# A recommendation kernel: the query of tile n-1 made between the masked and the weighted sums, gathers behind the products, both ends reordered

## The chip, the cores and the metric

The kernel runs on 1 core of one Trainium2 chip. The metric is the device time of one execution in microseconds (us). Three runs of the kernel before gave 188.56, 187.62 and 184.76 us, a median of 187.62 us.

## The reference, cut to what matters

512 users have 200 history rows of 128 floats each; a mask says which rows count.

```
maskf = mask;  decay = exp(-alpha * age) * maskf
mean  = (items * maskf).sum(1) / maskf.sum(1)             # [512, 128]
q     = mean @ Wq.T;  k = items @ Wk.T;  v = items @ Wv.T
scores = (q . k) / sqrt(128) + log(decay + 1e-12);  attn = softmax over unmasked rows
long  = attn @ v
short = mean of the 5 last valid rows;  g = sigmoid(gate of their mean popularity and age)
out   = layernorm(g * short + (1 - g) * long) * gamma + beta
```

The kernel multiplies Wq and Wk together once (`wqk`), so that a tile's "query" is the user's mean times `wqk` and is compared with the raw items; Wv is applied once per 128 users to the weighted sums.

## The kernel before, in words

**Tiles.** A tile is 16 users: 8 partitions per user, 25 rows of 128 floats on each partition, 1600 KB. There are 32 tiles in 10 buffers `x`; two tiles make a pair, four pairs a group of 128 users. SyncE issues the loads in order (L269 to L274); the load of tile n waits until the weighted sums of tile n-10 are done (`wx_done`).

**One tile, step by step.** TensorE makes masked sums (L430, with the mask blocks `mblk` from GpSimd, L321); ScalarE copies them scaled by the inverse counts (L581); TensorE folds them to the users' means (L454); ScalarE copies the mean (L596); TensorE makes the query (L463) in one of two PSUM banks, for which it first waits until VectorE has finished the tile before last (`dots_done`); ScalarE copies the query to SBUF (L605), which releases the scoring. The 25 rows are scored by two routes at once: VectorE does 17 of them, a multiply with a running sum each (`dots`, L879); GpSimd multiplies the other 8 in one instruction (`products`, L343) and ScalarE sums these row by row (`sum_products`, L570). VectorE then adds the log-decay and finds each user's maximum in five small steps strewn among the next dots (L826 to L852); ScalarE takes the exponential (L616); GpSimd lays the weights out in blocks (`pblk`, L332); TensorE makes the weighted sums (L438, L442), six slots behind the masked ones; ScalarE copies them (L590) and TensorE folds a pair into the group's bank (L477, L478).

**The order is written out by hand.** Every engine runs a function `slot(n)` for n = 0, 1, 2, ... (VectorE a `step` per pair), in program order, and they meet at semaphores only. TensorE's slot n is: masked sums of tile n, weighted sums of tile n-6, query of tile n-1, mean of tile n, fold of a pair; in the first slots the query comes ahead of the weighted sums. In slots 0 to 3 (`LEAD`) a tile's query is made in its own slot. ScalarE's slot n is: copy the weighted sums n-7, copy the mean n-1, the last four row sums of tile n-3, exponentials of a pair in odd slots, copy the masked sums n, the first four row sums of tile n-2, copy the query n-1. GpSimd's slot n: `pblk` of a pair or `mblk` of a pair, in turn, then the products of tile n-1. In the first slots GpSimd also issues eight small indirect loads of popularity and age (L410), two ahead of all slots and one per slot behind the products; once per group, in the slots 6, 14, 22 and 30, an indirect load of the last five rows (L383), with a copy of its offsets ahead of it (L380). The logarithm of the decay is taken by ScalarE in slot 1 (L623, L626), and VectorE's `setup_hide` (L758, L759) waits for it inside the dots of tile 2. VectorE has two more setup stretches (`setup_gate`, L770, and `setup_last_weights`, L787).

**Fillers.** `keep_busy` (L449) issues matmuls without use: 4 behind each of the slots 0 to 5, and in the last slots ahead of the weighted sums of the tiles 28 (8), 30 (3) and 31 (3). One such matmul is two instructions of the trace.

**Group end.** `sum_weights` (L506), the fold, `copy_att` (L636), `make_long` (L513), and VectorE's finish (L888 to L923); then the store of 64 KB.

## Time and profile before

| what | value |
|---|---|
| runs, median | 187.62 us (184.76 to 188.56) |
| the profiled execution | 185.52 us, span of the profile 183.8 us |
| busy PE / DVE / ACT / POOL | 86% / 83% / 66% / 78% of the span |
| mean granted TensorE clock | 0.956 |
| HBM read | 54.70 MB, 299 GB/s over the span |

PE is TensorE, PEld its weight loads, DVE VectorE, ACT ScalarE, POOL GpSimd, SPq the queue of SyncE. The shares are means over the span: all four engines are far busier in the middle than at both ends. The clock column tells the granted clock of TensorE as a share of 2.4 GHz, 0.50 being 1.2 GHz. A line of the timeline gives the start, the duration, and in brackets how long the engine sat idle before and who released it. Instructions of VectorE overlap by part of their length: 17 dots take 17 x 0.209 us from start to start, though each lasts 0.28.

### The profile page before, as it was taken

Reading aid. Unit: us, or ns where it says so; the run is one execution under the profiler, and the core shown is the slowest. Engines: PE = TensorE matmul, PEld = TensorE weight load, DVE = VectorE, ACT = ScalarE, POOL = GpSimd, SP = SyncE. Lnnn points to the kernel's source line nnn. Section 1 sums busy time; section 2 is a strip of 40 time slices with the busy share of each in tenths; the row PEclk is TensorE's granted clock in tenths of the full one; section 3 lists DMA queues with packets and bytes.
Section 4 is the critical chain, followed back from the end, with each engine's and each line's share of the span. In section 5 each row is a group of like instructions: output and inputs, shape, how many; then the busy total and the mean of one; then the engine's idle time right before and its main releaser. Section 6 shows DMA issues by size and latency. Waiting matters only on the chain.

```text
span 183.8 us, 8155 instructions
## 1 busy us (share of the span) xinstructions
PE 158.4 (86%) x2811; PEld 126.6 (69%) x2811; DVE 152.5 (83%) x1281; ACT 121.6 (66%) x714; POOL 144.1 (78%) x110
## 2 busy tenths in 40 slices
PE   5864649879969999999899999997999999497990
PEld 5753546767747688878686888876878878275660
DVE  4569719958893999999999999999999999979303
ACT  2021664747847599888778889894889889577210
POOL 5608967698899598999899999989999995974301
PEclk9999966999995799999999999999999999999997
DMA  4899999999999589999999999999999810200000
GB/s 105 288 416 378 334 423 412 397 416 419 405 368 358 233 306 427 362 362 379 407 428 424 370 382 407 401 410 395 405 399 366 350 35 0 77 16 0 4 0 14
DMA packets 8008, 55.48 MB, mean 302 GB/s; under 512 B 2080, under 2 KB 3360, under 8 KB 4000
## 3 DMA queue, kind: packets, MB, share of 16 engines
q1 hardware_dynamic: 7152, 53.59, 74.4%
q0 software_dynamic: 576, 1.33, 2.1%
q8 instruction: 22, 0.36, 0.8%
q14 instruction: 18, 0.15, 0.2%
q10 hardware_dynamic: 240, 0.05, 0.1%
HBM read 54.70 MB, written 0.26 MB: 299 GB/s over the span
## 4 chain that ended last, share of the span: by engine, by line
POOL 44%; PE 19%; issue 16%; ACT 12%; DMA 4%; DVE 1%; SPq 1%; POOLq 0%; ACTq 0%; DVEq 0%
POOL gprod L343 27%; ACT gprod L570 9%; POOL mblk L321 7%; PE ps_acc L430 7%; PE ps_acc L438 5%; POOL pblk L332 5%; DMA x<-in_r_hist_items_dram 4%; POOL taken L383 2%; PE ps_group L449 1%; PE ps_query L463 1%; ACT query L605 1%; PE ps_acc L454 1%; POOL pop_taken L410 1%; POOL age_taken L410 1%; PE ps_group L477 1%
## 5 line engine op out<-in xcount | busy, mean ns | idle before, releaser
L879 DVE SCALAR_TENSOR_TENSOR junk_v<-x,ps_query 128x128 f32<-128x128 f32 x544 | 121.2, 279 | 12.6 <-ACT query L605 12.5
L570 ACT ACTIVATE gprod<-gprod 128x128 f32<-128x128 f32 x256 | 75.7, 301 | 20.8 <-POOL gprod L343 20.3
L343 POOL TENSOR_TENSOR gprod<-x,query 128x1024 f32<-128x1024 f32 x32 | 76.1, 2379 | 12.0 <-ACT query L605 10.7
L430 PE MATMUL ps_acc<-x,mblk 128*16 128x128 f32 x1600 | 57.8, 282 | 3.2 <-DMA x<-in_r_hist_items_dram 2.7
L438 PE MATMUL ps_acc<-x,pblk 128*32 128x256 f32 x768 | 51.3, 384 | 7.2 <-POOL pblk L332 6.4
L430 PEld LDWEIGHTS ps_acc<-x,mblk 128*16 128x16 f32 x1600 | 46.5, 99 | 7.1 <-issue 3.1
L570 ACT ACTIVATION_READ_ACCUMULATOR gprod<-gprod 128x1 f32 x256 | 49.3, 193 | 0.0
L879 DVE DVE_READ_ACCUMULATOR junk_v<-x,ps_query 128x1 f32 x544 | 44.6, 82 | 0.0
L438 PEld LDWEIGHTS ps_acc<-x,pblk 128*32 128x32 f32 x768 | 27.3, 110 | 19.5 <-issue 6.0
L332 POOL TENSOR_TENSOR pblk<-own,ex 128x800 f32<-128x800 f32 (+1 forms) x17 | 25.1, 1475 | 4.5 <-ACT ex L616 4.4
L321 POOL TENSOR_TENSOR mblk<-own,mask_f 128x800 f32<-128x800 f32 (+1 forms) x17 | 24.9, 1468 | 0.2
L581 ACT ACTIVATE sums<-ps_acc,rcnt_rows 128x128 f32<-128x128 f32 x32 | 11.6, 361 | 14.6 <-PE ps_acc L430 14.5
L463 PE MATMUL ps_query<-wqk,mean_p 128*128 128x128 f32 x64 | 15.9, 330 | 1.9 <-ACT mean_p L596 1.5
L590 ACT ACTIVATE wx<-ps_acc 128x256 f32<-128x256 f32 x32 | 11.9, 371 | 8.1 <-PE ps_acc L442 8.1
L454 PE MATMUL ps_acc<-fold,sums 128*128 128x16 f32 x64 | 10.9, 246 | 6.6 <-ACT sums L581 6.5
L454 PEld LDWEIGHTS ps_acc<-fold,sums 128*128 128x128 f32 x64 | 10.0, 198 | 9.2 <-ACT sums L581 8.2
L463 PEld LDWEIGHTS ps_query<-wqk,mean_p 128*128 128x128 f32 x64 | 9.8, 191 | 8.3 <-issue 6.3
L449 PE MATMUL ps_group<-own_rows 128*128 128x128 f32 x74 | 13.1, 344 | 1.8 <-POOL own_rows L356 1.8
L449 PEld LDWEIGHTS ps_group<-own_rows 128*128 128x128 f32 x74 | 12.2, 255 | 1.8 <-POOL own_rows L356 1.8
L442 PE MATMUL ps_acc<-x,pblk 128*16 128x128 f32 x64 | 12.5, 277 | 0.0
L477 PE MATMUL ps_group<-fold,wx 128*128 128x16 f32 x64 | 12.4, 270 | 0.0
L478 PE MATMUL ps_group<-fold_odd,wx 128*128 128x16 f32 x64 | 12.4, 270 | 0.0
(112 smaller groups left out, 149.8 us busy)
## 6 DMA issues: line engine op xcount, KB each, us to landing
x<-in_r_hist_items_dram SPq DMA_DIRECT2D x31, 1600.0 KB, 9.0
x<-in_r_hist_items_dram SPq DMA_DIRECT2D x1, 832.0 KB, 7.9
x<-in_r_hist_items_dram SPq DMA_DIRECT2D x1, 768.0 KB
decay_s<-in_r_hist_age_hours_dram SPq DMA_DIRECT2D x4, 100.0 KB, 13.1
out_dram<-y SPq DMA_DIRECT2D x4, 64.0 KB, 4.3
mask_u<-in_r_hist_mask_dram SPq DMA_DIRECT2D x1, 100.0 KB, 7.2
wq<-in_L_rec_Wq_dram SPq DMA_DIRECT2D x1, 64.0 KB, 7.2
wk<-in_L_rec_Wk_dram SPq DMA_DIRECT2D x1, 64.0 KB, 7.5
```

Source lines behind the costliest of these rows:

```text
L321: nc.gpsimd.tensor_tensor(mblk[:, s % 2, t:t + tiles, :, :].rearrange("p t r u -> p (t r) u"), own[:, :].unsqueeze(1).broadcast_to([P, til ...
L332: nc.gpsimd.tensor_tensor(pblk[:, s % 2, t:t + tiles, :, :].rearrange("p t r u -> p (t r) u"), own[:, :].unsqueeze(1).broadcast_to([P, til ...
L343: nc.gpsimd.tensor_tensor(gprod[:, t, :].rearrange("p (r d) -> p r d", d=D), rows(at(s, t), DOTS, ROWS), query[:, s % 2, t, :].unsqueeze(1 ...
L430: ins = nc.tensor.matmul(dst[c:c + TU, 0:D], blk[:, s % 2, t, m, :], x[:, at(s, t), m * D:(m + 1) * D], start=(m < CG), stop=(m >= ROWS - CG))
L438: nc.tensor.matmul(dst[c:c + 2 * TU, 0:2 * D], blk[:, s % 2, t, m:m + 2, :].rearrange("p r u -> p (r u)"), x[:, at(s, t), m * D:(m + 2) * ...
L442: return nc.tensor.matmul(dst[c:c + TU, 0:D], blk[:, s % 2, t, m, :], x[:, at(s, t), m * D:(m + 1) * D], start=False, stop=True)
L449: nc.tensor.matmul(dst, turned, turned, start=True, stop=True)
L454: nc.tensor.matmul(mean_cols(s, t), sums[:, t, :], fold[:, :], start=True, stop=True).then_inc(mean_done, 1)
L463: nc.tensor.matmul(c_query[t], mean_p[:, t, :, :].rearrange("p u c -> p (u c)"), wqk[:, :], start=True, stop=True).then_inc(query_done, 1)
L477: nc.tensor.matmul(users, wx[:, s % 2, t, 0:D], fold[:, :], start=True, stop=False)
L570: ins = nc.scalar.activation(src, src, ACT.Copy, accum_out=score[:, s % 2, t, DOTS + r:DOTS + r + 1])
L879: ins = V.scalar_tensor_tensor(out=junk_v[:, t, r, :], in0=x[:, at(s, t), r * D:(r + 1) * D], scalar=1.0, in1=c_query[t], op0=ALU.mult, op ...
```

## The change

- `early = True`: TensorE makes the query of tile n-1 right behind the masked sums of tile n in every slot, ahead of the weighted sums of tile n-6.
- `LEAD` goes from 4 to 6: the tiles 4 and 5 also get their query in their own slot. In slot 6 no query and no products are made. ScalarE sums all eight product rows of the tile before in one go in these slots, and the exponentials of tiles 0 and 1 come at the end of slot 4.
- The logarithm of the decay moves from the end of slot 1 to slot 2, ahead of the row sums.
- GpSimd issues the eight small indirect loads two per slot in slots 0 to 3, behind the products, and no longer waits for the row numbers ahead of slot 0. The first group's load of rows moves from slot 6 to slot 4; all four read their offsets straight from `first_row`, without the copy and the wait on it.
- The last tile has 21 rows on VectorE and 4 on GpSimd and ScalarE. Its weight block is made by VectorE (`last_block`, ahead of `short_term` and `lay_out_sums`) in place of GpSimd. The block of tiles 28 and 29 is built in slot 32 ahead of the products of tile 31, and their exponentials come first in slot 33; the exponential of tile 30 comes ahead of the copy of the weighted sums 28.
- TensorE folds tiles 26 and 27 ahead of the weighted sums of tile 28, sums the weights behind those of tile 31, and the fillers ahead of tiles 30 and 31 are gone; those ahead of tile 28 go from 8 to 6.

```diff
 WX_BEHIND = 6
-LEAD = 4
+LEAD = 6
+LAST_TILE = NTILE - 1
 ROWS_AHEAD = 4
...
-DOTS = 17
+DOTS, DOTS_LAST = 17, 21
 GPROD = ROWS - DOTS
...
 POOL_OWN = 3
-BUSY_FIRST, BUSY_LEAD, BUSY_LAST = 13, 4, {NTILE - 4: 8, NTILE - 2: 3, NTILE - 1: 3}
+BUSY_FIRST, BUSY_LEAD, BUSY_LAST = 13, 4, {NTILE - 4: 6}
 def build(nc, items, mask, age, pop, Wq, Wk, Wv, gate_w, gate_b, gamma, beta, decay_alpha, out):
...
             return n if n < LEAD else n + 1
+
+        def dots_of(n):
+
+            return DOTS_LAST if n == LAST_TILE else DOTS
         def masked_blocks(n):
...
                     pool.wait_ge(gsums_done, (s - 1) * PAIR + t + 1)
-                nc.gpsimd.tensor_tensor(gprod[:, t, :].rearrange("p (r d) -> p r d", d=D), rows(at(s, t), DOTS, ROWS),
-                                        query[:, s % 2, t, :].unsqueeze(1).broadcast_to([P, GPROD, D]),
+                k = ROWS - dots_of(n)
+                nc.gpsimd.tensor_tensor(gprod[:, t, 0:k * D].rearrange("p (r d) -> p r d", d=D), rows(at(s, t), ROWS - k, ROWS),
+                                        query[:, s % 2, t, :].unsqueeze(1).broadcast_to([P, k, D]),
                                         ALU.mult).then_inc(gprod_ready, 1)
...
                     pool.wait_ge(short_part, g * LAST)
-                nc.gpsimd.tensor_copy(group_row[:, :], first_row[:, bass.ds(g, 1)]).then_inc(row_copied, 1)
-                pool.wait_ge(row_copied, g + 1)
-                pool.sem_inc(pool_passed, 1)
                 nc.gpsimd.indirect_dma_start(
                     out=taken[:, :, :].rearrange("p i d -> p (i d)"), out_offset=None, in_=items_rows,
-                    in_offset=bass.IndirectOffsetOnAxis(ap=group_row[:, :], axis=0)).then_inc(gathered, 16)
+                    in_offset=bass.IndirectOffsetOnAxis(ap=first_row[:, g:g + 1], axis=0)).then_inc(gathered, 16)
             def slot(n):
...
                 w = n - WX_BEHIND + 1
-                if tile(w) and w // PAIR == LAST_PAIR:
+                if n == NTILE:
+                    build_pblk(w + 1)
+                elif w == LAST_TILE - 1:
                     build_pblk(w, 1)
-                elif tile(w) and w % PAIR == 0:
+                elif tile(w) and w % PAIR == 0 and w // PAIR < LAST_PAIR - 1:
                     build_pblk(w)
...
                     products(n - 1)
-                if i == 6 and g < NGROUP:
+                if n < NGROUP:
+                    if n == 0:
+                        pool.wait_ge(rows_ready, 1)
+                    gather_context(2 * n)
+                    gather_context(2 * n + 1)
+                if n == NGROUP:
+                    gather(0)
+                if i == 6 and 0 < g < NGROUP:
                     gather(g)
-                if 1 <= n < 2 * NGROUP - 1:
-                    gather_context(n + 1)
             def gather_context(j):
...
                     in_offset=bass.IndirectOffsetOnAxis(ap=first_row[:, q:q + 1], axis=0)).then_inc(last_gathered, 16)
-            pool.wait_ge(rows_ready, 1)
-            gather_context(0)
-            gather_context(1)
             slots(slot)
...
                 keep_busy(wx_bank(s, t)[:, 3 * D:4 * D], BUSY_LAST.get(n, 0))
-                pe.wait_ge(pblk_ready, weighted_blocks(n))
+                if n == LAST_TILE:
+                    pe.wait_ge(last_block_ready, 1)
+                else:
+                    pe.wait_ge(pblk_ready, weighted_blocks(n))
                 sum_row_pairs(wx_bank(s, t), pblk, s, t, 1).then_inc(wx_done, 1)
...
                     nc.tensor.matmul(ps_group[:, 0:D], wq[:, :], wk[:, :], start=True, stop=True).then_inc(wqk_done, 1)
-                if i == 5 and g == NGROUP:
-                    sum_weights(g)
-                early = n < WX_BEHIND + LEAD
+                early = True
+                if n == NTILE + 2:
+                    fold_pair(w // PAIR - 1)
                 if early and tile(n - 1) and query_slot(n - 1) == n:
...
                     weighted_sums(w)
+                if w == LAST_TILE:
+                    sum_weights(g)
                 if not early and tile(n - 1) and query_slot(n - 1) == n:
...
                     make_query(*divmod(n, PAIR))
-                if tile(w - 1) and w % PAIR == 0:
+                if n != NTILE + 2 and tile(w - 1) and w % PAIR == 0:
                     fold_pair(w // PAIR - 1)
...
                     src = gprod[:, t, r * D:(r + 1) * D]
-                    ins = nc.scalar.activation(src, src, ACT.Copy,
-                                               accum_out=score[:, s % 2, t, DOTS + r:DOTS + r + 1])
-                if b == GPROD:
+                    at_row = dots_of(n) + r
+                    ins = nc.scalar.activation(src, src, ACT.Copy, accum_out=score[:, s % 2, t, at_row:at_row + 1])
+                if b == ROWS - dots_of(n):
                     ins.then_inc(gsums_done, 1)
...
                 copy_query(n)
+                if n == 2:
+                    log_decay()
                 if tile(n - 1):
                     sum_products(n - 1, 0, GPROD)
-                if n == 1:
-                    log_decay()
+                if n == 2 * PAIR:
+                    exponential(0)
+                    exponential(1)
             def slot(n):
+                w = n - WX_BEHIND - 1
                 if n < LEAD:
...
                     return
-                if tile(n - WX_BEHIND - 1):
-                    copy_weighted(n - WX_BEHIND - 1)
+                if n == NTILE + 1:
+                    exponential(n - 5)
+                    exponential(n - 4)
+                if n == NTILE + 3:
+                    exponential(LAST_TILE - 1)
+                if tile(w):
+                    copy_weighted(w)
+                if n == NTILE + 4:
+                    exponential(LAST_TILE)
                 if n >= SLOTS_OF_GROUP and n % SLOTS_OF_GROUP == SLOTS_OF_GROUP - 1:
...
                     copy_mean(n - 1)
-                if n > LEAD + 1 and tile(n - 3):
+                if n > LEAD + 1 and tile(n - 3) and dots_of(n - 3) == DOTS:
                     sum_products(n - 3, ROWS_AHEAD, GPROD)
-                if n % PAIR == 1 and PAIR * 2 < n < NTILE + PAIR:
+                if n % PAIR == 1 and n <= NTILE:
                     exponential(n - 5)
                     exponential(n - 4)
-                if n in (NTILE + 3, NTILE + 4):
-                    exponential(n - 5)
                 if tile(n):
...
                     turn_user_max(s, t)
+            def last_block():
+
+                dve.wait_ge(exp_done, NTILE)
+                dve.wait_ge(wx_done, NTILE - 2 * PAIR)
+                V.tensor_tensor(pblk[:, LAST_PAIR % 2, PAIR - 1, :, :], own_v.unsqueeze(1).broadcast_to([P, ROWS, TU]),
+                                ex[:, PAIR - 1, :].unsqueeze(2).broadcast_to([P, ROWS, TU]), ALU.mult
+                                ).then_inc(last_block_ready, 1)
+
             def lay_out_sums(s):
...
                                                  accum_out=score[:, k % 2, t, r:r + 1])
-                if a < b == DOTS:
+                if a < b == dots_of(s * PAIR + t):
                     ins.then_inc(dots_done, 1)
...
                 fin = has(g, 1, NGROUP)
-                for i in range(DOTS):
+                for i in range(dots_of(s * PAIR - 1)):
                     if i == 1 and k == 0 and has(g, 2, NGROUP):
...
                             if not has(s, 0) and fin and k == 0:
+                                last_block()
                                 for j in range(LAST):
```

## Rows read from the trace of the kernel before

**Rows 1.** The page's costliest group: count | busy, mean ns | idle before, releaser.

```profile
L879 DVE SCALAR_TENSOR_TENSOR junk_v<-x,ps_query 128x128 f32<-128x128 f32 x544 | 121.2, 279 | 12.6 <-ACT query L605 12.5
```
**Rows 2.** Windows: stretch, length, busy PE, PEld, DVE, ACT, POOL, clock, DMA share, GB/s.

```profile
24.00:28.00 4.00, 2.65 (x11) 2.54 (x12) 0.90 (x9) 2.42 (x11) 2.23 (x2) 0.54 1.01 413
56.00:60.00 4.00, 4.00 (x40) 3.31 (x39) 2.04 (x19) 3.51 (x23) 3.89 (x3) 0.50 0.96 355
60.00:64.00 4.00, 4.00 (x63) 2.42 (x51) 3.65 (x28) 1.82 (x12) 2.14 (x3) 0.76 0.60 242
64.00:68.00 4.00, 4.00 (x86) 3.29 (x86) 3.81 (x37) 3.61 (x22) 3.63 (x2) 1.00 0.75 253
100.00:104.00 4.00, 4.00 (x87) 3.46 (x83) 4.00 (x40) 3.30 (x21) 3.90 (x3) 1.00 0.98 407
```
**Rows 3.** Timeline, VectorE's waits: start, us, instruction, [idle before <-releaser].

```profile
27.10 0.29 DVE L879 SCALAR_TENSOR_TENSOR junk_v<-x,ps_query 128x128 f32<-128x128 f32 x1 [4.25 <-ACT query L605]
...
50.87 0.29 DVE L879 SCALAR_TENSOR_TENSOR junk_v<-x,ps_query 128x128 f32<-128x128 f32 x1 [1.14 <-ACT query L605]
...
57.96 0.29 DVE L879 SCALAR_TENSOR_TENSOR junk_v<-x,ps_query 128x128 f32<-128x128 f32 x1 [2.96 <-ACT query L605]
...
63.88 0.28 DVE L879 SCALAR_TENSOR_TENSOR junk_v<-x,ps_query 128x128 f32<-128x128 f32 x1
```
**Rows 4.** Timeline of the lead slots: GpSimd, ScalarE, TensorE.

```profile
17.98 4.68 POOL L343 TENSOR_TENSOR gprod<-x,query 128x1024 f32<-128x1024 f32 x2
...
18.84 0.28 ACT L605 ACTIVATE query<-ps_query 128x128 f32<-128x128 f32 x1 [0.58 <-PE ps_query L463]
19.63 1.69 PE L430 MATMUL ps_acc<-x,mblk 128*16 128x128 f32 x50
22.73 0.95 ACT L623 ACTIVATE decay_s<-decay_s,soft 128x800 f32<-128x800 f32 x1
24.58 0.35 ACT L581 ACTIVATE sums<-ps_acc,rcnt_rows 128x128 f32<-128x128 f32 x1
24.98 0.61 PE L454 MATMUL ps_acc<-fold,sums 128*128 128x16 f32 x2 [3.66 <-ACT sums L581]
28.15 2.21 DVE L758 TENSOR_TENSOR hide_s<-hide_s,decay_s 128x800 f32<-128x800 f32 x1
```
**Rows 5.** Loads of tiles 3 and 23, issue and landing; masked sums of tile 23.

```profile
L274 SPq DMA_DIRECT2D x<-in_r_hist_items_dram x1: 440/440/440, 8.2 to 8.2; - x1
DMA to landing us min/median/max: 17.6/17.6/17.6
...
L274 SPq DMA_DIRECT2D x<-in_r_hist_items_dram x1: 327/327/327, 105.6 to 105.6; - x1
DMA to landing us min/median/max: 8.9/8.9/8.9
...
118.58 1.59 PE L430 MATMUL ps_acc<-x,mblk 128*16 128x128 f32 x49
```
**Rows 6.** Timeline: a gather slot on GpSimd, and TensorE's masked sums at the lower clock.

```profile
122.32 1.05 POOL L383 DMA_INDIRECT taken<-in_r_hist_items_dram,group_row  x1 [0.82 <-PE ps_acc L442]
...
58.76 3.17 PE L430 MATMUL ps_acc<-x,mblk 128*16 128x128 f32 x50
```
**Rows 7.** Timeline from the slot ahead of the last products to the last pieces.

```profile
159.40 1.50 PE L438 MATMUL ps_acc<-x,pblk 128*32 128x256 f32 x24 [2.69 <-POOL pblk L332]
163.19 2.36 POOL L343 TENSOR_TENSOR gprod<-x,query 128x1024 f32<-128x1024 f32 x1 [1.08 <-ACT query L605]
165.51 1.55 POOL L332 TENSOR_TENSOR pblk<-own,ex 128x800 f32<-128x800 f32 x1
168.24 0.28 DVE L879 SCALAR_TENSOR_TENSOR junk_v<-x,ps_query 128x128 f32<-128x128 f32 x1
171.37 0.94 PE L449 MATMUL ps_acc<-own_rows 128*128 128x128 f32 x6
175.85 1.50 PE L438 MATMUL ps_acc<-x,pblk 128*32 128x256 f32 x24
```

9 lines of the change are left out of this document (4 added, 5 removed).

## The prediction

> **What bounds the kernel now.** I read the windows first. In the middle (100 to 104 us, and the stretches from 84 to 164 look alike) VectorE is busy in 4.00 us of 4, TensorE too, GpSimd in 3.90, the DMA share is 0.98 [rows 2]. So no share tells the bound, and I went to the waits. VectorE's dots waited 12.5 us in all for a query [rows 1], and the timeline has all but 0.5 us of that ahead of 58 us: 4.25 us ahead of the dots of tile 2, 1.14 ahead of tile 6, 2.96 ahead of tile 7 [rows 3], and 1.0 and 2.6 us between them (tiles 1 and 4). From 63.88 us, where the dots of tile 8 begin [rows 3], VectorE runs to the last ones at 168.24 [rows 7] with idle time of 1.6 us in all. **VectorE bounds the middle.** GpSimd and ScalarE hand each other products and queries in 4.0 us per tile just beside it, so nothing there can be won by a faster partner; but work that VectorE begins earlier at 64 us ends earlier at 168.
>
> The DMA is close behind. Its share is about 1 from 8 to 146 us but for 60 to 68 us, where it is 0.60 and 0.75 [rows 2], since TensorE was late with the sums that free buffers. Tile 23 lands at 114.5 us and is first read at 118.58 [rows 5]: 4.1 us to spare, the least that I found.
>
> After 168.5 us there is a serial end: maximum, exponential, block, weighted sums of tile 31 at 175.85 [rows 7], fold, last product, finish, store.
>
> **The start, slot by slot.** Pieces: masked sums 1.69 [rows 4]; from their end to the copied query 2.5 us, and 2.0 from the start of the copy of the sums (tile 1: 17.13 to 19.12 [rows 4]); products 2.36 [rows 7]; an indirect load 1.05 and 0.1 of issue [rows 6]; a block for two tiles 1.55 [rows 7]; eight row sums 2.35, four 1.2.
> - Slot 0: the products of tile 0 no longer stand behind two indirect loads and a block. They start with query 0 at 13.3, not 17.98 [rows 4], and end at 15.7.
> - Slot 1: query 1 is ready at 19.1, as before. ScalarE sums tile 0's products 19.1 to 21.5 and copies the sums of tile 2 at 21.5. Before, this copy stood behind sums that waited for the late products and behind the exponential and logarithm of the decay (22.73), and came at 24.58, with TensorE idle for 3.66 us and then at a clock of 0.54 [rows 2, 4]. Query 2 is ready at 23.5 instead of 27.1; the decay follows to 25.5.
> - VectorE: tile 2's dots from 23.6 stop at the decay (25.5), hide work 2.21 [rows 4], 1.75 and 0.37, end 33.1; tile 3 to 36.7, tile 4 to 40.8, tile 5 to 44.4 (3.6 a tile, 4.1 with the maxima).
> - Slots 3 to 5: tile 3 lands at 8.2 + 17.6 = 25.8 [rows 5], query 3 at 30.0; queries 4 and 5 at 34.6 and 39.7, ahead of VectorE's need.
> - GpSimd: products 1 19.1 to 21.5, two loads, block, products 2 to 28.0, two loads, products 3 to 32.7, two loads, block, products 4 to 39.0, rows load and block to 41.8, products 5 to 44.2.
> - Slots 6 and 7: masked 6 at 40.6, weighted 0 to 44.0, masked 7 44.3 to 45.9. ScalarE copies its sums at 46.0, does four row sums, and query 6 is ready at 47.9. **VectorE idles here**, 3.3 us. Dots of tile 6 then start 3.0 us earlier than 50.87.
> - Slot 8: query 7, now ahead of the weighted sums, is ready at 51.8, VectorE ends tile 6 at 52.0, so the 2.96 us ahead of tile 7 are gone. Tile 7 to 55.6, gate setup 2.4: tile 8 starts near 58.2 instead of 63.88. I take **5.5 us**. Low end 3.0 (tile 6's alone), high end 8.8 (5.5 and all of the new wait).
>
> What could take it back: tile 31's masked sums would come at 147.3 instead of 152.8. The load of tile 12 is issued when weighted sums 2 are done, near 53 instead of 56.6, so the hole of 1.6 + 1.0 us [rows 2] fills, and 4.1 + 2.6 = 6.7 us are to spare for 5.5. It just holds.
>
> **The middle.** The early query takes no work away. A new wait: the query of tile n-1 needs VectorE's dots of tile n-3, and the weighted sums of n-6 queue behind it, with the buffer that they free. Before, the query came 0.6 to 2.3 us after those dots, so TensorE will now stand here for up to 1.1 us; weighted sums then end 2.05 us after the dots, where they ended 0.7 to 2.7 after. TensorE needs 3.93 of 4.2 us a slot. Cost 0, covered by the second query bank; if uncovered, 1.1 us in each of some slots. The copy of the offsets went with 0.82 us of waiting [rows 6], three times on a GpSimd that VectorE does not wait for: about 0.3 us. The eight small loads are the same ones, only crowded; counted above.
>
> **The end**, counted from the dots of tile 31, which begin at the same point relative to all else. The exponentials 28 and 29 come at 163.1 to 163.8, and the block at 165.35, not 167.06 [rows 7]; products 31 have half the rows, and end at 166.6, 1 us later than before; ScalarE sums four to 167.9 and takes exponential 30 at 168.7, half a us earlier; weighted 28 and 29 run to 168.6, weighted 30 from 169.7 to 171.3, its fold to 172.2. VectorE's four more rows cost 4 x 0.209 = 0.84: end 169.35. Maxima 1.3, exponential 0.5: 171.3. The block on VectorE shows in no row. Bounds: 0.56 us from its small operations (slope between 50 and 128 elements), 1.1 from half of the 2.21 us one [rows 4]. I take 0.7, as it reads one operand from PSUM like the small ones. So weighted 31 start at 172.2, bound by fold and block alike, instead of 175.85. The sum of weights behind them costs 0.1. **3.5 us**. Low 1.85, the two fillers (0.94 and another like it [rows 7]); high 4.3.
>
> Fillers are also what kept the clock up. The trace has a fall to 0.54 right behind 3.66 us of idle TensorE [rows 2, 4], and another to 0.50 after idle pieces below 0.8 us each [rows 2], but none after 2.69 us idle at 156.7 to 159.4 [rows 7]. The Trainium skill (TensorE: Matmul & The Clock Gate, "Why this matters for your kernels") asks for no long idle stretch between bursts of matmuls and so speaks against dropping fillers; here the first fall agrees with it, the second does not follow it. By the rule the end would come near its rival below, by the rows it stays at 1.0, since the gaps I get there are 1 to 2 us.
>
> **Sum.** 5.5 + 3.5 = 9.0 us, the 0.3 left out. The profiled execution took 185.52 (span 183.8 and 1.7 around it): 176.5. The median of the runs lies 2.1 above it, at 187.62: **178.6 us**.
>
> **Rivals.**
> - *The start gives less*: 0.20. Wherever query 6 or 7 comes late again (the new wait shows how thin it is), or the clock falls at 53 to 62 us again, only tile 6's 3.0 remain, less 0.5: 187.6 - 2.5 - 3.5 = 181.6. For it: products, row sums and masked sums 7 all end within 2 us of each other there.
> - *The loads bind*: 0.07. If the DMA gives nothing back, the start is worth 4.1 at most: 187.6 - 4.1 - 3.5 = 180.0. Against it: the share falls to 0.60 exactly where buffers were late.
> - *The clock falls in the end*: 0.12 with its like. Four weighted sums at 1.50 each double, 6 us less 1 of idle: 187.6 - 5.5 - 3.5 + 5 = 183.6, no change. The same result if VectorE starves later and only the end is won: 184.1.
> - *Slower*: 0.06. The query's wait on the dots, ahead of the weighted sums, leaves TensorE short stops in every slot of the middle, and the clock falls there. Masked sums at half clock took 3.17 instead of 1.59 [rows 5, 6]; with the weighted ones a slot gets 2.4 us longer than VectorE's pace. Four such slots eat the 9.0; from six on it is slower by over 2%; with six, 187.6 - 9.0 + 14.4 = 193.0. Against it: all 4-us windows from 64 to 180 us had a clock of 1.00, with stops of 1 us in them.
> - *The query stays where it was in effect*: the moved instruction still waits for the same dots, so in the middle nothing changes. That is in the forecast.
>
> **Numbers.** Forecast 0.55, the others as above. The runs of before spread by 3 us below and 1 above their median's value, and the start is unsure by 2: 174.5 at the low end. Above, 181.6 is to be held, and a run's spread: 183.0. Within 2% (183.9 to 191.4) is what a measurement of this kernel can hardly tell from no change. Faster 0.82, within 0.12, slower 0.06.
>
> **What would show it.** ScalarE's copy of tile 2's sums at 21.5 and no clock below 0.9 at 24 to 32; a wait of about 3 us of VectorE on query 6 and none on query 7; its dots of tile 8 at 58; a DMA share near 1 at 60 to 68; from there to the last dots again about 105 us, 0.8 of it for the four rows; GpSimd's waits of 0.82 gone; weighted 31 some 3 us after the last dots instead of 7.3. I am wrong if VectorE waits for queries between 64 and 160, if TensorE waits for loads, or if the clock column shows less than 1 in the middle.

## The result and the profile after

The kernel after the change takes **188.4 us** (median of 5 runs, 187.56 to 189.5), the kernel before beside it 187.39 (184.22 to 188.56). The ratio is 1.021, with a 95% interval of 1.016 to 1.025: **slower**, by about 2%, where 178.6 us and a faster kernel had been forecast. Some executions of a kernel take a few per cent longer than its others at a lower granted clock: the ratios in this document leave them out, and the profiles of fill_narrow, lead7 and lead7_copy, further down, are of such executions. The profiled execution took 188.13 us (span 186.4), that of before 185.52 (span 183.8).

Three marks cut both spans: the first dots of tile 8, the first dots of tile 31, the end. The span is printed to a tenth, so the last part is good to 0.05 us. The forecast was given for the three parts one by one.

```
                       start   middle   end    span
before                 63.88    99.27   20.65  183.8
after                  59.06   103.19   24.15  186.4
forecast, change        -5.5      0      -3.5
measured, change        -4.8     +3.9    +3.5
```

The start came nearly as forecast. The middle, forecast at no cost, lost 3.9 us, and the end went 7 us to the wrong side. First the page of after: sections 1, 4 and 5 (the head of the chain of waits, and the costliest group, which answers to [rows 1]).

```profile
PE 164.9 (88%) x2795; PEld 125.6 (67%) x2795; DVE 156.6 (84%) x1290; ACT 123.3 (66%) x706; POOL 141.7 (76%) x105
...
PE 60%; POOL 16%; issue 15%; DMA 4%; DVE 2%; ACT 2%; SPq 1%; POOLq 0%
...
L907 DVE SCALAR_TENSOR_TENSOR junk_v<-x,ps_query 128x128 f32<-128x128 f32 x548 | 121.8, 278 | 7.0 <-ACT query L616 6.9
```

VectorE's waits for queries fell from 12.5 to 6.9 us. But 3.1 of the 6.9 are new: 0.36, 1.19, 0.37 and 1.19 us at 102.67, 121.08, 138.82 and 157.22 us, where before had 0.46 in the same stretch. A wait for queries between 64 and 160 us was one of the forecast's signs that it is wrong. The chain that ended last is now 60% TensorE; in the page of before it was 44% GpSimd and 19% TensorE. An engine that the forecast had called covered has become the bound.

The windows of after (stretch, length, busy time of PE, PEld, DVE, ACT and POOL, clock, DMA share, GB/s), to be held against [rows 2]:

```profile
8.00:12.00 4.00, 2.83 (x51) 1.95 (x52) 2.47 (x7) 0.49 (x3) 1.98 (x2) 0.76 1.08 406
12.00:16.00 4.00, 3.63 (x22) 3.17 (x26) 3.22 (x19) 0.84 (x3) 1.50 (x1) 0.50 0.98 416
24.00:28.00 4.00, 2.51 (x58) 2.05 (x56) 3.01 (x11) 3.97 (x17) 3.99 (x3) 1.00 0.99 405
60.00:64.00 4.00, 4.00 (x78) 3.09 (x80) 4.00 (x40) 3.65 (x24) 3.85 (x2) 1.00 1.02 427
100.00:104.00 4.00, 4.00 (x88) 2.87 (x84) 3.64 (x33) 3.10 (x20) 3.02 (x3) 1.00 0.94 356
164.00:168.00 4.00, 0.03 (x1) 0.03 (x1) 2.92 (x28) 1.88 (x12) 2.28 (x3) 0.88 0.06 16
168.00:172.00 4.00, 4.00 (x20) 3.66 (x24) 3.02 (x26) 0.41 (x2) 0.87 (x1) 0.50 0.00 0
```

At 24 and at 60 us the clock is 1.00, where before it was 0.54 and 0.76 [rows 2], and the hole in the DMA share at 60 us is filled. At 100 us VectorE is down from 4.00 to 3.64 and GpSimd to 3.02, while TensorE stays at 4.00. And at 164 us TensorE stands for a whole window and then runs at the lower of its two levels (0.50 is 1.2 of 2.4 GHz). Two questions, then: what fills TensorE in the middle, and what stops it at 164 us.

**The middle.** The timeline of TensorE in one slot of after (start, us, line, operation), from the mean matmul (L460) of the slot ahead of it up to its own:

```profile
102.82 0.40 PE L460 MATMUL ps_acc<-fold,sums 128*128 128x16 f32 x2
103.14 1.70 PE L436 MATMUL ps_acc<-x,mblk 128*16 128x128 f32 x50
104.77 0.49 PE L469 MATMUL ps_query<-wqk,mean_p 128*128 128x128 f32 x2
105.19 1.50 PE L444 MATMUL ps_acc<-x,pblk 128*32 128x256 f32 x24
...
106.82 0.40 PE L460 MATMUL ps_acc<-fold,sums 128*128 128x16 f32 x2
```

And the same of before, up to the masked sums (L430) of the next slot:

```profile
136.77 1.59 PE L430 MATMUL ps_acc<-x,mblk 128*16 128x128 f32 x49
138.09 0.39 PE L438 MATMUL ps_acc<-x,pblk 128*32 128x256 f32 x3
138.20 0.27 PE L430 MATMUL ps_acc<-x,mblk 128*16 128x128 f32 x1
138.31 1.46 PE L438 MATMUL ps_acc<-x,pblk 128*32 128x256 f32 x21
...
139.70 0.49 PE L463 MATMUL ps_query<-wqk,mean_p 128*128 128x128 f32 x2
140.03 0.29 PE L454 MATMUL ps_acc<-fold,sums 128*128 128x16 f32 x2
140.25 1.70 PE L430 MATMUL ps_acc<-x,mblk 128*16 128x128 f32 x50
```

The instructions are the same; the starts are not. Before, weighted sums begin 1.32 us after masked ones, while the last masked sum is still to come (x49, x3, x1, x21: the two kinds mix). From the start of the masked sums to the start of the query, both kinds of sums together take 2.93 us. After, the query starts only at the end of the masked sums (1.63 us behind their start), the weighted sums follow it after 0.42, and the mean comes 1.63 later: 3.26 us for the sums. Query and mean, side by side before at 0.33 and 0.22, now stand alone at 0.42 and 0.32. In sum 0.33 + 0.09 + 0.10 = **0.52 us more per slot**. A slot without a wait goes from 3.48 to 4.00 us, and one with a fold from 4.37 to 4.90. The 21 slots 10 to 30, from the masked sums of tile 10 to those of tile 31, take 95.2 us, where they took 88.6 with their waits.

**The end.** TensorE of after from the fold (L483) of tiles 26 and 27 on:

```profile
167.97 0.61 PE L483 MATMUL ps_group<-fold,wx 128*128 128x16 f32 x2 [4.14 <-ACT wx L601]
...
168.85 2.91 PE L455 MATMUL ps_acc<-own_rows 128*128 128x128 f32 x12
171.69 2.57 PE L444 MATMUL ps_acc<-x,pblk 128*32 128x256 f32 x24
...
178.42 1.50 PE L444 MATMUL ps_acc<-x,pblk 128*32 128x256 f32 x24
```

What it and VectorE waited for, by the timelines of GpSimd, ScalarE and VectorE of after:

```profile
162.97 1.54 POOL L336 TENSOR_TENSOR pblk<-own,ex 128x800 f32<-128x800 f32 x1 [3.33 <-ACT ex L627]
164.48 0.57 POOL L355 TENSOR_TENSOR rstd<-vare,half 128x1 f32<-128x1 f32 x1
165.03 1.25 POOL L348 TENSOR_TENSOR gprod<-x,query 128x512 f32<-128x512 f32 x1
...
166.38 0.31 ACT L582 ACTIVATE gprod<-gprod 128x128 f32<-128x128 f32 x1 [2.04 <-POOL gprod L348]
...
167.56 0.36 ACT L601 ACTIVATE wx<-ps_acc 128x256 f32<-128x256 f32 x1
...
165.08 0.35 DVE L951 SCALAR_TENSOR_TENSOR y<-ps_dve,rstd,bet 128x128 f32<-128x128 f32 x1 [2.54 <-POOL rstd L355]
...
176.78 0.58 DVE L892 TENSOR_TENSOR pblk<-ps_dve,ex 128x400 f32<-128x400 f32 x1 [5.52 <-ACT ex L627]
```

Read it backwards; rstd is the inverse deviation that ends a group's layernorm. The fold at 167.97 waits for the copy of weighted sums 27. ScalarE has that copy at 167.56, behind the four row sums of tile 31, which wait for the last products. Those stand on GpSimd behind the block and behind rstd (L355). Behind the fold, on TensorE, queue weighted 28 to 31, whose first block was ready at 164.5. Before, that fold came behind weighted 28. The second stop is VectorE's: 2.54 us ahead of 165.08, behind the first dot of tile 31, for the same rstd. Weighted 31 start 16.2 us behind the first dots of tile 31 (178.42 less 162.25). Before had 12.7 (175.85 [rows 7] less 163.15), and the forecast, which counted from the same dots as before, 9.05 (172.2 less 163.15).

### The profile page after: what moved, and what is told of

The parts are those of the page before. It is cut to its first block, busy times and chain, and to the rows that moved or that the text cites. A ratio compares the mean times of both kernels' runs of the same rounds, so it can differ in the third digit from the quotient of the medians.

```text
span 186.4 us, 8117 instructions
## 1 busy us (share of the span) xinstructions
PE 164.9 (88%) x2795; PEld 125.6 (67%) x2795; DVE 156.6 (84%) x1290; ACT 123.3 (66%) x706; POOL 141.7 (76%) x105
## 4 chain that ended last, share of the span: by engine, by line
PE 60%; POOL 16%; issue 15%; DMA 4%; DVE 2%; ACT 2%; SPq 1%; POOLq 0%
PE ps_acc L436 22%; PE ps_acc L444 18%; POOL gprod L348 7%; PE ps_query L469 6%; PE ps_acc L460 4%; DMA x<-in_r_hist_items_dram 4%; PE ps_group L484 3%; PE ps_group L483 3%; PE ps_acc L448 2%; POOL pblk L336 2%; POOL pop_taken L419 2%; POOL mblk L325 2%; POOL age_taken L419 2%; DVE junk_v L907 1%; POOL taken L385 1%
## 5 line engine op out<-in xcount | busy, mean ns | idle before, releaser
L348 POOL TENSOR_TENSOR gprod<-x,query 128x1024 f32<-128x1024 f32 (+1 forms) x32 | 74.8, 2336 | 14.5 <-ACT query L616 13.0
L582 ACT ACTIVATE gprod<-gprod 128x128 f32<-128x128 f32 x252 | 74.1, 301 | 3.1 <-POOL gprod L348 2.9
L436 PE MATMUL ps_acc<-x,mblk 128*16 128x128 f32 x1600 | 56.0, 277 | 2.9 <-DMA x<-in_r_hist_items_dram 2.9
L444 PE MATMUL ps_acc<-x,pblk 128*32 128x256 f32 x768 | 49.2, 390 | 0.2 <-POOL pblk L336 0.2
L582 ACT ACTIVATION_READ_ACCUMULATOR gprod<-gprod 128x1 f32 x252 | 48.5, 193 | 0.0
L444 PEld LDWEIGHTS ps_acc<-x,pblk 128*32 128x32 f32 x768 | 22.6, 111 | 15.2 <-issue 1.6
L336 POOL TENSOR_TENSOR pblk<-own,ex 128x800 f32<-128x800 f32 (+1 forms) x16 | 24.1, 1508 | 8.8 <-ACT ex L627 8.7
L460 PEld LDWEIGHTS ps_acc<-fold,sums 128*128 128x128 f32 x64 | 9.7, 191 | 10.4 <-issue 5.5
L483 PE MATMUL ps_group<-fold,wx 128*128 128x16 f32 x64 | 12.3, 267 | 4.8 <-ACT wx L601 4.8
L460 PE MATMUL ps_acc<-fold,sums 128*128 128x16 f32 x64 | 12.9, 276 | 3.4 <-ACT sums L592 3.4
L483 PEld LDWEIGHTS ps_group<-fold,wx 128*128 128x128 f32 x64 | 9.9, 195 | 5.6 <-ACT wx L601 5.2
L355 POOL TENSOR_TENSOR rstd<-vare,half 128x1 f32<-128x1 f32 x4 | 2.3, 566 | 13.9 <-DVE vare L940 13.9
```

The costliest lines, as they stand in the source:

```text
L336: nc.gpsimd.tensor_tensor(pblk[:, s % 2, t:t + tiles, :, :].rearrange("p t r u -> p (t r) u"), own[:, :].unsqueeze(1).broadcast_to([P, til ...
L348: nc.gpsimd.tensor_tensor(gprod[:, t, 0:k * D].rearrange("p (r d) -> p r d", d=D), rows(at(s, t), ROWS - k, ROWS), query[:, s % 2, t, :].u ...
L436: ins = nc.tensor.matmul(dst[c:c + TU, 0:D], blk[:, s % 2, t, m, :], x[:, at(s, t), m * D:(m + 1) * D], start=(m < CG), stop=(m >= ROWS - CG))
L444: nc.tensor.matmul(dst[c:c + 2 * TU, 0:2 * D], blk[:, s % 2, t, m:m + 2, :].rearrange("p r u -> p (r u)"), x[:, at(s, t), m * D:(m + 2) * ...
L460: nc.tensor.matmul(mean_cols(s, t), sums[:, t, :], fold[:, :], start=True, stop=True).then_inc(mean_done, 1)
L483: nc.tensor.matmul(users, wx[:, s % 2, t, 0:D], fold[:, :], start=True, stop=False)
```

## The experiments

Theory M: the middle is longer because TensorE takes longer over the same instructions, since a query between masked and weighted sums breaks their overlap. Rival M2 is the forecast's own: the query's wait on VectorE's dots makes the stops. Theory E: the end is long by the order of the moved work (fold ahead of weighted 28, rstd behind the block); rival E2: it is long by TensorE's clock, which fell since fillers were dropped. The expectations call M and E theory A, and M2 and E2 theory B. Each ratio is to before in the same job, with its 95% interval; the three marks are those of the profiled execution.

**Each part taken back, or done alone.** Label mid_late: the change, the query late from slot 10 on.

```diff
-                early = True
+                early = n < 10
```

> The changed kernel with one line put back: from slot 10 on the query of tile n-1 stands behind the weighted sums again. Theory A (order of shapes): a matmul on the whole array between two runs of sums on a part of its columns costs TensorE about 0.5 us a slot, as the trace shows 4.01 us for a slot without a fold where it showed 3.48. TensorE then binds the middle. It expects 3.48 and about 4.4 us a slot again, 99.3 us from VectorE's first dots of tile 8 to its first dots of tile 31 instead of 103.2, and a total 3.5 to 4.5 us below the changed kernel (about 184). Theory B (the query waits for VectorE's dots of tile n-3, and the weighted sums queue behind it): in both orders the same wait stands in front of the query, so the slots of TensorE grow with stops in them; it expects idle gaps of TensorE in the changed kernel's middle, and that they go with the line put back. Theory C (the extra 3.9 us of the middle come from GpSimd, ScalarE or the loads): no change, 103 us in the middle.

Measured: ratio 0.989 (0.984 to 0.994), middle 98.39, end 24.44. The whole middle came back, 4.8 us, by one line, and the end stayed long. Label before_early is the mirror: before, with `early = True`.

> The kernel before with the query ahead of the weighted sums in every slot, and nothing else. Theory A expects slots of 4.0 and 4.9 us on TensorE from slot 10 on, 103 us from the dots of tile 8 to those of tile 31 instead of 99.3, and a total 3.5 to 4.5 us longer than before (about 191.5), with the clock at 1.00 in the middle. Theory B expects less, as VectorE starts later here: 0 to 2 us. If the loss needs the new start (theory C), the time stays at 187.4.

Measured: 1.024 (1.017 to 1.030), middle 103.01 (+3.7), slots 4.01 and 4.90 as in after, end 20.15. So the early query costs the middle about the same with or without the rest of the change.

Label start_only: before, with LEAD = 6, the query late from slot 10, the small gathers two per slot behind the products of slots 0 to 3, the first load of rows in slot 4 and all four without the copy of the offset, the decay in slot 2 and the first exponentials in slot 4.

> The kernel before with the new start alone: query of tiles 4 and 5 in their own slot, indirect loads behind the products, no copy of the offsets, the decay in slot 2; the query is early in the slots up to 9 as before, late from 10 on, and the end is that of before (all tiles 17 rows on VectorE). Expected if the start is worth what VectorE's dots of tile 8 show (59.06 instead of 63.88 us): those dots at 59 us, 99.3 us on to tile 31's, the end 20.6 us behind them: 4.8 us off, about 182.6. Rival (what is won at the start is taken back in the middle by the loads or by GpSimd whatever the order on TensorE): 185 to 187, with a stop of VectorE or of TensorE on a load.

Measured: 0.967 (0.958 to 0.976), profiled 179.09; first dots of tile 8 at 59.83, middle 98.39, end 19.18. The start is sound by itself, and gives more than expected (median 179.04 for about 182.6): the middle is 0.9 us shorter than before's, as in mid_late, and the end, where no order was edited, 1.5. The traces show where the 1.5 lie. GpSimd of before, then of start_only, around the last load of rows:

```profile
153.27 2.39 POOL L343 TENSOR_TENSOR gprod<-x,query 128x1024 f32<-128x1024 f32 x1 [1.61 <-ACT query L605]
...
157.70 1.56 POOL L332 TENSOR_TENSOR pblk<-own,ex 128x800 f32<-128x800 f32 x1
```

```profile
147.69 2.39 POOL L343 TENSOR_TENSOR gprod<-x,query 128x1024 f32<-128x1024 f32 x1 [1.61 <-ACT query L604]
...
151.28 1.56 POOL L332 TENSOR_TENSOR pblk<-own,ex 128x800 f32<-128x800 f32 x1
```

From the products to the block behind the load it is 4.43 us in before and 3.59 without the copy and its wait. Counted from the first dots of tile 31, that block starts 5.45 us ahead in before and 6.94 in start_only, and the pieces of the end that follow are all 1.5 us earlier. No run takes out the copy alone, so this is read from the traces and not isolated.

Label tail_fold_rstd: the change, with the fold behind the weighted sums in all slots, and rstd ahead of the block.

```diff
-                if n == NTILE + 2:
-                    fold_pair(w // PAIR - 1)
...
-                if n != NTILE + 2 and tile(w - 1) and w % PAIR == 0:
+                if tile(w - 1) and w % PAIR == 0:
...
+                if i == 0 and has(g, 2, NGROUP):
+                    inverse_deviation(g - 2)
...
-                if i == 0 and has(g, 2, NGROUP):
-                    inverse_deviation(g - 2)
```

> The changed kernel with two things of the end put back: the fold of tiles 26 and 27 stands behind the weighted sums of tile 28 again, and on GpSimd the inverse deviation of group 2 stands ahead of the block of tiles 28 and 29. Theory A (order in the end): the block was ready at 164.5 us, but TensorE stood for 4.1 us in front of the fold, which waits for ScalarE's copy of weighted sums 27, behind the late products of tile 31; and VectorE stood 2.5 us in front of a finish that waits for GpSimd. It expects VectorE's wait of 2.54 us gone, weighted sums 28 right behind their block, and 4.5 to 6 us off the total: about 183. Theory B (the missing fillers and the lower clock behind the idle stretch are the cause, the order is not): the clock still falls, as TensorE still idles, and at most 2.4 us come back.

Measured: 0.986 (0.978 to 0.993), end 17.89 where after had 24.15. Its TensorE at the same places:

```profile
162.50 1.60 PE L455 MATMUL ps_acc<-own_rows 128*128 128x128 f32 x12
164.64 1.50 PE L444 MATMUL ps_acc<-x,pblk 128*32 128x256 f32 x24 [0.54 <-POOL pblk L336]
...
167.51 0.40 PE L483 MATMUL ps_group<-fold,wx 128*128 128x16 f32 x2 [0.63 <-ACT wx L599]
...
172.20 1.50 PE L444 MATMUL ps_acc<-x,pblk 128*32 128x256 f32 x24
```

The stops of 4.14 and 2.54 us are down to 0.63 and under 1 us, the 12 fillers take 1.60 instead of 2.91, the clock is 1.00 from 160 to 176 us, and weighted 31 start at 172.20, which is 9.9 us behind the first dots of tile 31 (162.31). Two kernels split the repair. Label tail_fold has the fold's part alone:

> The changed kernel with only the fold of tiles 26 and 27 put back behind the weighted sums of tile 28; on GpSimd the inverse deviation still stands behind the block. The two repairs together gave 182.1 us. If the fold was nearly all of it: VectorE's wait of 2.54 us stays, but weighted 28 start at 164.5, the clock stays at 1.00, and the total is 182.5 to 184, bound by the last dots. If GpSimd's order was the larger part: 186 or more.

Measured: 0.987 (0.980 to 0.995), end 18.45, the clock at 1.00 throughout the end. Label tail_rstd has the part of rstd alone:

> The changed kernel with only GpSimd's order put back: the inverse deviation of group 2 ahead of the block of tiles 28 and 29; the fold stays ahead of the weighted sums of tile 28. VectorE's wait of 2.54 us should shrink to about 1 (for the row sums of tile 30), and the products of tile 31 come 0.5 us earlier, and with them ScalarE's copy that the fold waits for. If TensorE's fold binds the end, as the runs with both repairs (an end of 17.9 us behind the first dots of tile 31) and with the fold alone (18.5) say, only 0.5 to 1 us come back: an end of 23.2 to 23.7 instead of 24.15. If VectorE's wait was on the path by itself, 2 us or more.

Measured: 1.010 (1.002 to 1.018), end 23.96; TensorE still stands 3.60 us at the fold. By the ends, the fold's place is worth 5.7 us, the place of rstd 0.2 alone and 0.6 behind the other.

**What the early query costs TensorE.** Three kernels leave before's order alone and add one unread whole-array matmul or a narrow one per slot; no semaphore is touched, so no new wait on dots can come in. Label fill_between: the matmul (two instructions, 128 stationary columns, as the query) between masked and weighted sums, in the slots with weighted tiles 4 to 25.

```diff
-                keep_busy(wx_bank(s, t)[:, 3 * D:4 * D], BUSY_LAST.get(n, 0))
+                keep_busy(wx_bank(s, t)[:, 3 * D:4 * D], BUSY_LAST.get(n, 1 if n >= 4 and n < NTILE - 6 else 0))
```

> The kernel before with one useless matmul on the whole array (two instructions) between the masked and the weighted sums in the slots 10 to 31; the query stays behind the weighted sums. It waits for nothing of VectorE. Theory A (a matmul on the whole array between two runs of sums on a part of the columns breaks their overlap) expects TensorE's slots to grow by the matmul itself, 0.2 to 0.3 us, and 0.3 us more, to about 4.0 and 4.9 us: a middle of 102 to 103.5 us instead of 99.3 and a total about 3 us above before. Theory B (the query's wait for the dots is what costs) expects only the matmul's own time, hidden behind VectorE: no change, a middle of 99 to 100.

Label fill_beside: the same matmul directly ahead of the query's (`if 9 <= s * PAIR + t < NTILE - 1: keep_busy(...)`).

> The kernel before with the same useless matmul in the same slots, but right ahead of the query behind the weighted sums, where matmuls on the whole array stand anyway. The same added work as in the run with the matmul between the sums. Theory A expects 0.2 to 0.3 us a slot on TensorE and no more: slots of about 3.7 and 4.6, 4.2 on average, just VectorE's pace: a middle of 99 to 100.5 us and a total 0 to 1 us above before. If it costs as much as between the sums (3 us), the place does not matter and theory A falls: then any work added to TensorE costs its price.

Label fill_narrow: between masked and weighted sums again, but with 16 stationary columns, as the masked sums have.

> The kernel before with one useless matmul between the masked and the weighted sums in the slots 10 to 31, as in the run with the filler between the sums (193.4 us, slots of 4.23 and 5.12), but its stationary operand has 16 columns and its output 16 partitions, like a masked sum's, instead of 128. Theory A as stated (it is the matmul on the whole array that breaks the overlap of the masked with the weighted sums, since it needs all the columns that the sums before and behind it use) expects slots of about 3.6 and 4.5 us, a middle of 99 to 100.5 us and the time of before. Theory D (any foreign matmul between the two, or its other PSUM area, breaks it) expects slots above 4.0 and 4.9 and 3 to 8 us more than before.

```
               slot, slot with fold   added per slot   middle   ratio to before
before          3.48    4.37             -              99.3    -
fill_between    4.23    5.12            0.75           107.2    1.044 (1.036 to 1.052)
fill_beside     3.70    4.59            0.22           101.5    1.012 (1.005 to 1.019)
fill_narrow     3.69    4.59            0.21           103.4    1.007 (1.002 to 1.012)
after           4.01    4.90            0.53           103.2    1.021 (1.016 to 1.025)
```

The slots are those without a wait. The middle of fill_narrow is not compared with the others; its slots and its ratio are. TensorE of fill_between, then of fill_narrow, in one slot:

```profile
115.67 0.49 PE L449 MATMUL ps_acc<-own_rows 128*128 128x128 f32 x2
116.09 1.50 PE L438 MATMUL ps_acc<-x,pblk 128*32 128x256 f32 x24
...
117.72 0.49 PE L463 MATMUL ps_query<-wqk,mean_p 128*128 128x128 f32 x2
...
118.27 1.70 PE L430 MATMUL ps_acc<-x,mblk 128*16 128x128 f32 x50
```

```profile
123.23 0.27 PE L430 MATMUL ps_acc<-x,mblk 128*16 128x128 f32 x1
123.34 0.27 PE L499 MATMUL ps_acc<-own_rows,own 128*16 128x128 f32 x1
123.37 0.39 PE L438 MATMUL ps_acc<-x,pblk 128*32 128x256 f32 x3
...
123.56 1.24 PE L438 MATMUL ps_acc<-x,pblk 128*32 128x256 f32 x17
```

The same two instructions cost 0.22 us beside the query and 0.75 between the sums. The difference, 0.53, is after's loss per slot to the hundredth. The narrow one mixes with both kinds of sums and costs 0.21 in the very place where the wide one costs 0.75. So it is neither the work nor the place alone, but a matmul over the whole array (128 stationary columns) between two runs of matmuls that use a part of its columns. Two expectations were too low. For fill_between the break had been put at 0.3 us, and with 0.53 the middle came out at 107.2 instead of 102 to 103.5. For fill_beside 0 to 1 us had been expected and a middle of up to 100.5; it is 101.5, so that even 0.22 us a slot is not covered by VectorE's pace.

The Trainium skill says of this (TensorEngine Tiling (Array Packing), "Key Properties") that a change of the tiling mode, as against a change of the tile, drains TensorE. The three rows agree with it, if matmuls over the whole array and over a part of its columns are two such modes; by these runs two extra changes in a slot cost 0.53 us.

**Is the end the clock's?** Label tail_fill: the change as it is, with 60 filler instructions ahead of the early fold (and none in slot 28), so that TensorE does not stand.

> The changed kernel with 30 useless matmuls ahead of the fold of tiles 26 and 27 in slot 34 (60 instructions, some 4 us at the upper clock) and none ahead of the weighted sums of tile 28. They fill the stretch in which TensorE stood idle for 4.14 us and keep its clock up; the order of the end stays that of the change. Theory A (the order costs, the clock little) expects the clock at 1.00 at 168 to 176 and at most 2.5 to 3 us off, as the 12 instructions of filler (2.91 us) go and the weighted sums 28 take 1.5 instead of 2.57 us: about 185.5. Theory B (the clock is what costs) expects all of the lost 6 us back: about 182.5.

Measured: 1.002 (0.999 to 1.006), end 21.55. Its fillers on TensorE's timeline with the fold behind them, ScalarE's copy that the fold needs, and the window at 168 us, where after fell to 0.50:

```profile
163.64 6.96 PE L455 MATMUL ps_acc<-own_rows 128*128 128x128 f32 x60
170.44 0.29 PE L483 MATMUL ps_group<-fold,wx 128*128 128x16 f32 x2
...
168.78 0.36 ACT L602 ACTIVATE wx<-ps_acc 128x256 f32<-128x256 f32 x1
```

```profile
168.00:172.00 4.00, 4.00 (x44) 3.72 (x46) 3.82 (x36) 1.55 (x9) 0.87 (x1) 1.00 0.01 4
```

With the clock at 1.00 throughout the end, 2.6 us of after's 6.3 come back, where E2 expects all of them. The 2.6 are not the clock's price, though: the 60 fillers took 6.96 us and not the expected 4, so that the fold starts 7.0 us behind the first dots of tile 31 (163.45), against 5.7 in after, though its copy was done at 169.14; and after's 12 fillers went with the edit. An estimate of the price goes by rows at either clock, after against tail_fold_rstd: the 12 fillers 2.91 and 1.60, weighted 28 2.57 and 1.50, from the fold to what follows its pair 0.88 and 0.55, in sum 2.7 us. The rest of the 6.3 is order. And the clock fell by the order: tail_fold adds no filler, moves the fold alone, and has its clock at 1.00 and 5.7 us back. E holds, and the fall that E2 speaks of is its consequence.

**Together, and further.** Label all_three: the change with the edits of mid_late and tail_fold_rstd, which is start_only with the change's end, repaired.

> The changed kernel with the query behind the weighted sums from slot 10 on, the fold of tiles 26 and 27 behind the weighted sums of tile 28, and the inverse deviation ahead of the block on GpSimd: the three repairs together. If they are independent: first dots of tile 8 near 58.5 us, a middle of 98.4, an end of 17.9: a span near 175 us, a time near 177.5, 8.5 us below before and 2 below the new start alone. If the loads bind once TensorE no longer does: a middle over 100 us with waits of TensorE on loads, and 179 or more.

Measured: 0.955 (0.949 to 0.961), the three marks 59.67, 98.38 and 17.85. The same kernel in another job, label all_three_again:

> The three repairs again, to have them on the same chip as the two runs beside it: 95 to 96.5% of the time of before, an end of 17.9 us.

Measured: 0.954 (0.949 to 0.959), profiled 175.98. Label all_three_copy moves the copy of weighted 27 ahead of the row sums of tile 31 on ScalarE:

```diff
-                if tile(w):
+                if tile(w) and n != NTILE + 2:
...
+                if n == NTILE + 1:
+                    copy_weighted(w + 1)
```

> The three repairs, and ScalarE's copy of weighted sums 27 ahead of the row sums of tile 31. With the longer lead this end took 17.1 us instead of 17.8. Expected: an end of 17.1 to 17.2 us and 0.5 to 0.9 us less than the three repairs alone; the start as there.

Measured: **0.950 (0.944 to 0.956)**, median 176.33, end 17.06. Its interval overlaps the one of all_three_again, so that it is the better of the two is shown by the end in the profile (0.8 us), not by the times.

Last, the stop of VectorE ahead of tile 6. Label lead7 is all_three with LEAD = 7, lead7_copy has the copy's edit too, lead7_again repeats lead7.

> The kernel with all three repairs (177.4 us), and the lead one slot longer: tile 6 too gets its query and its products in its own slot, before which VectorE still stood 3.49 us. Expected: query 6 some 2 to 2.5 us earlier, of which the first dots of tile 8 keep 1 to 2, a time of 175.5 to 176.5. Rival: TensorE stands in slot 6 for the copies of ScalarE and is as much later in slot 7, so that tile 7's query comes late instead: no change.

> The same with one more edit: ScalarE copies weighted sums 27 in slot 33 ahead of the row sums of tile 31, which wait for GpSimd, instead of behind them. TensorE's stop of 0.62 us in front of the fold goes, and weighted sums 29 start about 0.85 us earlier. Expected 0.6 to 0.9 us below the run with the longer lead alone, if VectorE's block of the last tile (then 0.1 to 0.3 us ahead of need) holds; if it is late, 0.3 less.

> The three repairs with a lead of 7 slots. If VectorE's stop in front of query 6 was the loss and a longer lead cures it: 1 to 2 us less than the three repairs alone. If TensorE only pays elsewhere for its wait in slot 6 (the longer wait of VectorE in front of query 7, 2.4 us in the run before): no change or up to 1.5 us more.

Measured: 0.967 (0.959 to 0.975), 0.980 (0.973 to 0.987, from two executions) and 0.958 (0.953 to 0.964). The gain of 1 to 2 us over all_three that the first of them was expected to bring did not come. Only the third's profile is read. VectorE's waits there:

```profile
49.80 0.21 DVE L844 TENSOR_TENSOR kept<-score,ps_dve 128x50 f32<-128x50 f32 x1 [1.54 <-ACT ex L625]
...
54.09 0.29 DVE L905 SCALAR_TENSOR_TENSOR junk_v<-x,ps_query 128x128 f32<-128x128 f32 x1 [1.82 <-ACT query L614]
```

The stop ahead of tile 6, 2.31 us in all_three_again, is gone and stands as 1.54 and 1.82 us behind it. One more tile of lead moves the stop and removes nothing.

## Why the prediction was wrong

**The middle is the step that failed first.** It said that the early query takes no work away, that TensorE needs 3.93 of 4.2 us a slot, and that the cost is 0. The 3.93 is right for before, (3.48 + 4.37) / 2. It was carried over to after as if it were a property of the instructions; there it is (4.01 + 4.90) / 2 = 4.46, above VectorE's pace (4.2 in the forecast; 4.28 by the middle of mid_late, 98.39 us for 23 tiles). By the forecast's own numbers the cover was 0.27 us a slot, and the cost was 0.53. The slot of 4.0 us stood in before's own trace, since before makes the query early up to slot 9. Its TensorE there:

```profile
41.97 1.70 PE L430 MATMUL ps_acc<-x,mblk 128*16 128x128 f32 x50
43.60 0.49 PE L463 MATMUL ps_query<-wqk,mean_p 128*128 128x128 f32 x2
44.02 1.50 PE L438 MATMUL ps_acc<-x,pblk 128*32 128x256 f32 x24
...
45.97 0.63 PE L430 MATMUL ps_acc<-x,mblk 128*16 128x128 f32 x16
```

From masked to masked 4.00 us, against 3.48 late in the trace. The forecast took a slot's work as the same in either order, and never set a slot of the one order beside a slot of the other. By this row the middle would have come out at 21 x 0.53 = 11 us of work less 21 x 0.27 of cover, 5.5 us; measured was 3.9, or 4.8 beside the middles of mid_late and start_only. TensorE's 21 slots grew by 6.6 us, more than the middle did. The likely difference is the lead that it had over VectorE, whose first wait for a query behind tile 8 comes only at 102.67 us; no run isolates it.

**The end** failed as well: forecast 3.5 us won, measured 3.5 lost. The block on VectorE was well estimated (0.7 us, 0.58 measured), and with the order repaired the end is won, but by less than forecast: 17.9 us instead of 20.6, so 2.7. That weighted 31 then start at 172.20, where 172.2 was forecast, is luck: the dots of tile 31 begin 0.84 us earlier there than in before, and counted from them it is 9.9 us, not 9.05. Against start_only, which keeps before's order in the end and has 19.2, the repaired order is worth 1.3. What the step left out is the order that the diff writes: that the fold of tiles 26 and 27 moved ahead of weighted 28 on TensorE's queue while its operand stays behind tile 31's row sums on ScalarE's, and that rstd, moved behind the block, is awaited by VectorE amid its last dots. The forecast asked of the moved query what it waits for; of the moved fold and rstd it did not.

**The start** held: 4.8 us for 5.5, in one pair of profiles. ScalarE copied tile 2's sums at 22.26 (21.5 forecast), VectorE waited 2.30 us for query 6 (3.3) and not for query 7, and its tile 8 began at 59.06 (58.2). The clock stayed at 1.00 at 24 us, but fell to 0.50 at 12 us, where before had 1.00. That may account for the missing 0.7: tail_rstd and tail_fold_rstd have the same start, their clock stayed at 1.00 up to there, and tile 8 began at 57.50 and 58.12 (58.2 forecast). In tail_fold, again the same start, it began only at 61.53; so the size of this gain goes with the execution, and 4.8 is one value of it. The forecast left out the gathers without the offset's copy at 0.3 us, on a GpSimd that VectorE does not wait for. By start_only they are worth up to 0.9 in the middle and up to 1.5 in the end, where GpSimd is waited for.

**The rivals.** The slower one, given 0.06, named the right stretch and sign and the wrong mechanism: short stops behind the wait on the dots, a falling clock, 193.0. In after, TensorE has no idle time over 0.25 us between 44 and 157 us, and its clock is 1.00 in every window there. Three kernels without any new wait lose in the same way, so this rival fell, and so did the statement that the query stays where it was in effect. That the clock falls in the end came true (0.50 at 168 us), but for a stop of 4.14 us that the forecast did not have; its share is about 2.7 us by the estimate above. The forecast had seen in the fillers what kept the clock up; but tail_fold_rstd has no fillers ahead of tiles 30 and 31 either, and its clock stayed at 1.00. The Trainium skill (TensorE: Matmul & The Clock Gate, "Why this matters for your kernels"), quoted in the forecast for asking that no long idle stretch stand between bursts, is borne out by that stop. The forecast said that by this rule the end would come near the rival; but the gaps of 1 to 2 us that it had there are no long stretches, so the rule did not say so. The clock was not what decided. The loads did not bind: the last wait of TensorE for a load is 1.19 us at 26 us.

The sum, put right with these sizes: 185.52 - 4.8 + 3.9 + 3.5 = 188.12, and the profiled execution took 188.13. The marks cut the whole span, so this agrees by construction and proves nothing more.

## What to carry to other kernels

Price a moved instruction by a whole slot in the new order against one in the old, start to start; look whether the kernel already runs the new order somewhere. On TensorE, keep matmuls over the whole array next to each other and don't put one between runs that use a part of the columns. When an instruction is moved forward on its queue, look up where its operand stands on the queue of the engine that makes it, for everything behind it now waits for that too.

## What the runs showed of the hardware

- A whole-array fp32 matmul of two instructions costs 0.22 us of a slot beside another (fill_beside), 0.75 between two runs of matmuls with 16 and 32 stationary columns (fill_between); one of 16 columns costs 0.21 there (fill_narrow). Matmuls of 16 and of 32 columns overlap: weighted sums start 1.32 us behind masked ones that last 1.59.
- The granted clock fell to 0.50 behind 4.14 us of idle TensorE. It was 0.76 and 0.50 at 8 to 16 us of after too, where the idle pieces ahead of that were 1.85 us at the very start, 0.52 and 1.17, and it did not fall behind 2.69 us in before [rows 7]. So the longest stop alone does not tell whether it falls. Kernels with the same start differed in this: tail_rstd had no fall there.
- A 128x400 product with one operand in PSUM took VectorE 0.58 us (after, L892).
